# Attention weights turned compact and set on the diagonal by DMA, with the patch products moved

## The chip, the cores and the metric

One core of a Trainium2 chip. Its engines run side by side and wait for each other by semaphores: PE (TensorE, matrix products, results in PSUM), DVE (VectorE), ACT (ScalarE), POOL (GpSimd), and SP (SyncE), whose queue issues most DMA transfers. The metric is the device time of one launch in microseconds (us), the median of several runs.

## What is computed

A vision transformer layer on 64 images: patches are embedded (36 patches and one class token, so 37 tokens of 256), attention with 16 heads of 64, a layer norm, a mixture of 8 experts with two chosen per token plus a shared feed-forward part, and a second layer norm. Cut to what the change touches:

```python
def _L0_attn_ref(x, Wq, Wkv, Wout, b_out, pos_emb):
    B, N, D = x.shape                      # 64, 37, 256
    ...
    sim = jnp.einsum('bid,bjd->bij', q, k) * scale
    sim = sim + _cope(q, sim, pos_emb)
    attn = jax.nn.softmax(sim, axis=-1)    # 37 x 37 for each image and head
    out = jnp.einsum('bij,bjd->bid', attn, v)
    ...
    return out @ Wout + b_out
```

Everything is in float32.

## The kernel before

**Tiling.** Three images make a group `g` of 111 rows (3 x 37); there are 22 groups, the last with one image. Two groups make a pair `p` (0 to 10): groups `2p` (called `a = 0` or `ga`) and `2p + 1` (`a = 1` or `gb`). Pairs 2 to 9 run as a hardware loop or in the same form; pair 0, pair 1 and pair 10 are written apart. After pair 10 come the router and the shared part (PE lines 1060 to 1293), then the experts in tiles of 128 tokens (lines 1360 and 1372), then the second norm and the output.

**One pair on PE**, in the order in which it is written by hand (`pair` in the tensor block): `queries(p)` (line 878), `score(p, 0)` (957), `values(p, 0, ·)` (971), `turn_weights(2p - 1)` (993), `values(p, 1, ·)`, `outputs(2p - 1)` (1006), `score(p, 1)`, `embed(p + 1)` (869, the patch products), `residual(p - 1)` (1015), `keys(p + 1)` (878), `turn_weights(2p)`, `by_tokens(p - 1)` (1031), `outputs(2p)`. Each engine runs its own list in its own order; a semaphore wait stops everything that stands behind it on that engine.

**How the attention weights get to the output product.** `softmax_norm` on DVE (lines 1888 to 1900) sums the exponentials `ex`, takes the reciprocal, multiplies it by `own_f` (one where a row belongs to image `b`, zero elsewhere), and writes `attn[row, head, image, token]`, 111 x 16 x 111, in four parts of four heads: so each head's 111 x 111 block is zero outside the three 37 x 37 diagonal blocks. PE turns each head by a product with the identity (16 of them a group), ACT copies the four banks to `attnT` (line 1476), and PE multiplies the values `v_sb` by `attnT`, one product a head, 111 rows deep.

**Around it.** ACT takes every PSUM result away: `score` (three copies one after another, 1435 to 1439), `values` (1470), `gates` (1455 and 1457, what the next scan on DVE starts from), `outputs` (1491), `keys` (1420), `queries` (1415), `split` (1524), `softmax_exp` (1499). DVE carries `cope`, the position term, in seven parts for each group: a scan (1827) that waits for `gates`, shifted copies by predicate (1844), and arithmetic up to `lg` (1868), from which ACT takes the exponential. `embed(p + 1)` on DVE (1815) stands behind part 7 of `cope(ga)`. DVE's first step for group `ga` is `tables_out` (1912), which waits for `score(p, 0)` on PE. SP issues `save_h` (574), `store_rows` (562), `store_halves` (569), `load_x` (557), `turn_x` (610, a transposing DMA) and `back_h` (582) for each pair; behind the loop it loads the rows for the router (`load_rec`, 641) and the experts' weights (656, 659).

## Time and profile before

| | |
|---|---|
| median of 3 runs | 718.61 us (717.4 to 719.63) |
| the profiled execution's own time | 717.29 us |
| its span, first to last instruction | 715.5 us |
| mean granted PE clock | 0.994 |
| busy: PE, DVE, ACT, POOL | 98%, 73%, 61%, 17% |

Of the span, pairs 0 to 10 take about 477 us, the rest of the router and the shared part runs to 540 us, the experts to 657 us. The profile's views used below are: the timeline (start, length, engine, line, what is written from what, and in square brackets how long the engine sat idle before it and who ended that), the busy time in given stretches (which also gives the granted PE clock, 1.00 being 2.4 GHz and 0.50 being 1.2 GHz), the list of the instructions of one tile, and the DMA view.

### The profile page before, as it was taken

The numbers are of one execution on the slowest core, as the hardware profiler recorded it, in microseconds if no ns is written. First come the engines' busy times: TensorE is split into PE (matmuls) and PEld (weight loads), VectorE is DVE, ScalarE is ACT, GpSimd is POOL, SyncE is SP. The second block draws the span as 40 slices with busy tenths as digits, with TensorE's granted clock in tenths as the row PEclk, the third lists the DMA queues.
The fourth block names the chain that finished last, engine by engine and source line by source line (L and its number), as shares of the span: only waits on it lengthen the run. The fifth ranks groups of instructions, "written<-read, shape, count | busy, mean of one in ns | idle before, by whom it ended". The sixth has DMA issues, their size and how long they took to land. (4 is left out here: it accounts for less than half of the span.)

```text
span 715.5 us, 14500 instructions
## 1 busy us (share of the span) xinstructions
PE 698.0 (98%) x4930; PEld 606.4 (85%) x4931; DVE 524.1 (73%) x1109; ACT 437.4 (61%) x772; POOL 122.0 (17%) x158
## 2 busy tenths in 40 slices
PE   8999999999999999999999999989998999999995
PEld 5897897979889797988979796868887999998884
DVE  3378998989989898989989898986862222332657
ACT  1565777676776867677686747543216777784453
POOL 2000000000000000000000000010024777775130
PEclk9999999999999999999999999989999999999999
DMA  8620040402304040210402003920004655542811
GB/s 272 225 64 0 2 102 26 102 20 43 76 13 102 25 101 25 61 53 13 94 21 64 25 25 115 345 77 25 3 26 97 146 136 132 147 130 57 287 69 54
DMA packets 75659, 60.79 MB, mean 85 GB/s; under 512 B 49386, under 2 KB 66896, under 8 KB 75628
## 3 DMA queue, kind: packets, MB, share of 16 engines
q1 hardware_dynamic: 71056, 50.35, 26.0%
q0 software_dynamic: 4224, 9.71, 5.1%
q8 instruction: 17, 0.28, 0.2%
q10 hardware_dynamic: 348, 0.34, 0.1%
q14 instruction: 14, 0.11, 0.0%
HBM read 35.40 MB, written 15.54 MB: 71 GB/s over the span
## 5 line engine op out<-in xcount | busy, mean ns | idle before, releaser
L1360 PEld LDWEIGHTS ps_S<-attnT,v_sb 128*128 128x128 f32 x704 | 84.8, 192 | 5.8 <-ACT attnT L1691 3.4
L1360 PE MATMUL ps_S<-attnT,v_sb 128*128 128x128 f32 x704 | 85.8, 275 | 2.5 <-ACT attnT L1691 2.5
L1844 DVE COPY_PREDICATED table<-bit,table 111x112 f32<-111x112 int16 (+6 forms) x110 | 75.0, 682 | 11.2
L775 POOL TENSOR_TENSOR rs<-ve,neg_half 111x2 f32<-111x2 f32 x11 | 12.2, 1113 | 402.4 <-DVE ve L1936 402.4
L971 PE MATMUL ps_X<-wkv_sb,hT 128*111 128x512 f32 (+1 forms) x176 | 80.6, 598 | 0.0
L2280 DVE COPY attnT<-ps_S 128x256 f32<-128x256 f32 x44 | 18.7, 424 | 80.9 <-PE ps_S L1372 80.8
L1015 PE MATMUL ps_X<-oT,wout_sb 128*128 128x222 f32 x320 | 62.0, 350 | 0.0
L1015 PEld LDWEIGHTS ps_X<-oT,wout_sb 128*128 128x128 f32 x320 | 60.0, 190 | 0.0
L878 PE MATMUL ps_S<-hT,wq_sb 128*128 128x216 f32 (+1 forms) x320 | 59.2, 342 | 0.0
L971 PEld LDWEIGHTS ps_X<-wkv_sb,hT 128*111 128x111 f32 (+1 forms) x176 | 28.5, 173 | 35.0 <-issue 34.2
L878 PEld LDWEIGHTS ps_S<-hT,wq_sb 128*128 128x128 f32 x320 | 56.1, 189 | 1.3
L794 POOL DMA_INDIRECT attn<-hh_d,ids_x x44 | 45.2, 1026 | 60.6 <-issue 57.0
L1711 ACT COPY v_sb<-gu_sb 128x1024 f32 x44 | 45.7, 1038 | 12.2 <-issue 8.1
L957 PE MATMUL ps_S<-kT,qT 64*111 64x150 f32 (+1 forms) x704 | 50.5, 293 | 0.0
L957 PEld LDWEIGHTS ps_S<-kT,qT 64*111 64x111 f32 (+1 forms) x704 | 45.0, 170 | 5.5 <-issue 2.9
L1900 DVE TENSOR_TENSOR attn<-ex,rdo 111x444 f32<-111x444 f32 x84 | 46.5, 615 | 2.4
L808 POOL DMA_INDIRECT y_d<-attnT,ids_y x44 | 44.7, 1017 | 18.3 <-issue 10.7
L869 PE MATMUL ps_X<-patT,tokT 128*128 128x216 f32 x240 | 47.7, 353 | 0.0
L869 PEld LDWEIGHTS ps_X<-patT,tokT 128*128 128x128 f32 x240 | 44.2, 188 | 1.7 <-issue 1.7
L1372 PE MATMUL ps_S<-down_sb,q 128*128 x176 | 45.2, 380 | 0.3 <-DVE q L2274 0.3
L1691 ACT COPY attnT<-table 128x512 int16<-128x512 int16 x44 | 33.7, 766 | 18.8 <-DMA table<-attn 18.7
L993 PEld LDWEIGHTS ps_S<-ident,attn 111*111 111x111 f32 x336 | 35.7, 177 | 10.1 <-DVE attn L1900 6.3
(319 smaller groups left out, 1391.4 us busy)
## 6 DMA issues: line engine op xcount, KB each, us to landing
down_sb<-in_x_dram SPq DMA_DIRECT2D x10, 648.0 KB
gu_sb<-y_d SPq DMA_DIRECT2D x8, 512.0 KB, 6.5
h_d<-hT SPq DMA_DIRECT2D x11, 222.0 KB, 2.6
kept<-h_d SPq DMA_DIRECT2D x11, 222.0 KB, 2.8
h_d<-h SPq DMA_DIRECT2D x10, 222.0 KB
wkv_sb<-in_L_attn_Wkv_dram SPq DMA_DIRECT2D x2, 1024.0 KB, 12.5
gu_sb<-in_L_ffn_gate_w_dram SPq DMA_DIRECT2D x2, 1024.0 KB, 9.7
gu_sb<-in_L_ffn_up_w_dram SPq DMA_DIRECT2D x2, 1024.0 KB, 11.1
```

The source lines that it names most:

```text
L794: nc.gpsimd.indirect_dma_start(xg[:, b], None, hh_d[:, :], bass.IndirectOffsetOnAxis(ap=ids_x[:, t:t + 1], axis=0), bounds_check=REAL - 1, ...
L808: nc.gpsimd.indirect_dma_start(y_d[:, :], bass.IndirectOffsetOnAxis(ap=ids_y[:, t:t + 1], axis=0), y_sb[:, b], None, bounds_check=TOPK * R ...
L869: mm = nc.tensor.matmul(embedded(p, m), tokT[:, k, m * P:(m + 1) * P], pt[:, k % 2, :, :, k // 2, :], start=(k == 0), stop=(k == KP - 1))
L878: mm = nc.tensor.matmul(bank[:, i * NPAT:i * NPAT + n * (TOK - 1)], w[:, k, c:c + P], hT[:, k, :n, 1:], start=(k == 0), stop=(k == KE - 1))
L957: mm = nc.tensor.matmul(S[lane:lane + r, bank, col:col + KW], qT[part, f, a * ROWS:a * ROWS + r], kT[part, f, a], start=True, stop=True)
L971: mm = nc.tensor.matmul(X[:r, 1 - s], hT[:, k].rearrange("p b t -> p (b t)")[:, a * ROWS:a * ROWS + r], wkv_sb[:, k, INNER + 512 * s:INNER ...
L1015: mm = nc.tensor.matmul(bank[:, m * COLS:m * COLS + w], wout_sb[:, f, m * P:(m + 1) * P], oT[:, f, :w], start=(f == 0), stop=(f == FT - 1))
L1360: mm = nc.tensor.matmul(S[:, i, j * FF + f * P:j * FF + f * P + P], held[:, i, k, j, f * P:f * P + P], xgT[:, i, k], start=(k == 0), stop= ...
L1372: mm = nc.tensor.matmul(E[:, i, :EMB], hid[:, i, k * P:(k + 1) * P], down_sb[:, bass.ds(e, 1), k].rearrange("p o f -> p (o f)"), start=(k ...
L1711: nc.scalar.copy(held[:, i].rearrange("p k j f -> p (k j f)"), gu_sb[:, bass.ds(e, 1)].rearrange("p o k j f -> p (o k j f)")).then_inc(til ...
L1844: A.did(V.copy_predicated(near[:, :, :, 0:SL - d], by_side(bit[:, n], r)[:, :, :, 0:SL - d], near[:, :, :, d:SL]))
L1900: V.tensor_tensor(attn[:r, of], ex[:r, of].unsqueeze(2).to_broadcast(by_head), rdo[:r, of].unsqueeze(3).to_broadcast(by_head), ALU.mult).t ...
```

## The change

**Compact weights.** DVE writes the softmax without zeros: one product `attn[row, head, token]`, 111 x 16 x 37, with each head padded to 40 columns (`own_attn`). `own_f` and its product are gone. PE turns three heads at a time: 120 columns become 120 rows, in 6 products with the identity a group (five of three heads, one of a single head) where there were 16. ACT copies two banks of three products each to `turned_attn` (two copies of 120 x 333 for four of 111 x 444). Nine DMAs on SP (`place_attn`), each of 40 rows and 6 or 5 heads (888 or 740 bytes a row), then set the three images' blocks on the diagonal of `own_T`, which lies in `attnT`, 120 rows deep. POOL zeroes `attnT` once. `outputs` waits for the nine (`placed[a]`). The values (`v_sb`, `hT`, `kept`, `h_d`) get the same padding to 40 tokens an image, 120 rows a group; the last group, with one image, keeps the old form.

**Order.** PE: `embed(p + 1)` now stands ahead of `outputs(2p - 1)`, writing to bank `S[:, 2]`; `turn_weights(2p)` stands behind the first of the four key products; `outputs(2p)` moves into the next pair, ahead of the fourth query product; for group 0 it stands behind `patches(2)`, for group 20 behind three products of the shared part. ACT: `weights(2p - 1)` ahead of `gates(p, 0)`; `softmax_exp(2p)` ahead of `gates(p, 1)`; `distance(2p)` and `halves_of_x` earlier; the two halves of `turned_patches` among the query copies of the next pair. DVE: `embed(p + 1)` behind part 4 of `cope(ga)` instead of part 7. SP: the nine transfers of each group, and behind the loop the experts' weights after them.

On ACT, in the loop, between the copies of the scores and the gates. `v_sb` is a copy of value products, `th` and `gate` are the gates. Before:

```order
L1439 COPY simS<-ps_S 37x666
L1470 COPY v_sb<-ps_X 111x512
L1455 ACTIVATE th<-simS 111x592
L1457 ACTIVATE gate<-th 111x16x37
L1470 COPY v_sb<-ps_X 111x512
```

and after:

```order
L1487 COPY simS<-ps_S 37x666
L1518 COPY v_sb<-ps_X 120x512
L1523 ISA
L1524 COPY attn<-ps_S 120x3x111
L1523 REGISTER_ALU
L1524 COPY attn<-ps_S 120x3x111
L1503 ACTIVATE th<-simS 111x592
L1505 ACTIVATE gate<-th 111x16x37
L1518 COPY v_sb<-ps_X 120x512
```

Two copies of turned weights, with their waits for PE, now stand between the scores and the gates.

On PE, in the loop, from the turned weights of `gb` to the second score. Before:

```order
L993 MATMUL ps_S<-ident,attn 111x111 x4
L967 REGISTER_ALU
L971 MATMUL ps_X<-wkv_sb,hT 111x512 x4
L1006 MATMUL ps_S<-attnT,v_sb 64x111 x16
L957 MATMUL ps_S<-kT,qT 111x150 x6
```

and after:

```order
L1036 MATMUL ps_S<-ident,attn 120x111 x5
L1036 MATMUL ps_S<-ident,attn 40x111
L1009 REGISTER_ALU
L1014 MATMUL ps_X<-wkv_sb,hT 120x512 x4
L907 ISA
L911 MATMUL ps_S<-patT,tokT 128x216 x12
L1053 MATMUL ps_S<-attnT,v_sb 64x111 x16
L999 MATMUL ps_S<-kT,qT 111x150 x6
```

The patch products (`patT,tokT`) now lie between the value products and the output products.

On SP, in the loop, from the load of the next patches (`load_x`) to the end of the loop's body. Before:

```order
L555 REGISTER_ALU
L557 ISA
L557 DMA down_sb<-in_x_dram 108x1536
L608 ISA
L610 DMA_TRANSPOSE gu_sb<-down_sb 128x24x112
L579 ISA
L582 DMA kept<-h_d 128x444
```

and after:

```order
L645 DMA_TRANSPOSE gu_sb<-down_sb 128x24x112
L631 REGISTER_ALU
L632 ISA
L637 DMA attnT<-attn 40x222 x3
L637 DMA attnT<-attn 40x185 x6
L599 ISA
L602 DMA kept<-h_d 128x480
```

The nine transfers of a group stand ahead of `back_h`, behind a wait for ACT's copies.

The diff, cut to its core:

```diff
+            def place_attn(p, a):
+                g = p * 2 + a
+                if first(g):
+                    sp.wait_ge(attnT_zeroed, 1)
+                else:
+                    sp.wait_ge(o_done, g * 2)
+                sp.wait_ge(at_sb, g * 4 + 4)
+                apart(sp)
+                for j in range(TPG):
+                    n, at = in_block[j], from_slot[j]
+                    for b in range(TPG):
+                        sp.dma_start(own_T[PAD * b:PAD * b + PAD, b, at:at + n], turned_attn[PAD * j:PAD * j + PAD, b, :n]
+                                     ).then_inc(placed[a], 16)
...
             with sp.Fori(2, G2 - 4) as p:
                 save_h(p)
                 store_rows(p - 2)
+                place_attn(p - 1, 1)
                 store_halves(p - 2)
                 load_x(p + 3, XR)
                 turn_x(p + 2)
+                place_attn(p, 0)
                 back_h(p)
...
             for c in range(4, FULL):
                 load_rec(c)
+            place_attn(G2 - 2, 1)
             store_halves(G2 - 3)
+            back_h(G2 - 1)
+            place_attn(G2 - 1, 0)
+            store_rows(G2 - 2)
+            load_rec(FULL)
...
             def queries(p, ahead):
...
+                    if s == 3 and not next_first(p):
+                        outputs(p * 2 - 2, 0)
...
             def keys(p):
...
+                    if s == 1 and not next_first(p):
+                        turn_weights(p * 2 - 2, True)
...
             def turn_weights(g, ahead):
...
-                for j, s in enumerate(IN_TURN):
-                    pe.wait_ge(attn_ready, g * 4 + j + 1)
-                    for i in range(4):
-                        mm = nc.tensor.transpose(S[:r, s, i * r:i * r + r], attn[:r, 4 * s + i], ident[:r, :r])
-                    mm.then_inc(at_done, 1)
+                pe.wait_ge(attn_ready, g * 4 + 4)
+                for n in range(BLOCKS):
+                    heads_in = attn_flat[:r, heads_of(n)]
+                    mm = nc.tensor.transpose(S[:heads_in.shape[1], n // 3, n % 3 * r:n % 3 * r + r], heads_in, ident[:r, :r])
+                    if n % 3 == 2:
+                        mm.then_inc(at_done, 2)
...
             def outputs(g, a):
                 r = rows_of(g)
+                if r == ROWS:
+                    pe.wait_ge(placed[a], (g - a) * (8 * PLACES) + 16 * PLACES)
...
             def first_pair():
...
-                pe.wait_ge(q_sb, 4 + 2)
+                pe.wait_ge(q_sb, 4 + 3)
                 turn_weights(0, True)
+                values(1, 0, 0)
                 pe.wait_ge(q_sb, 4 + 4)
-                outputs(0, 0)
+                pe.wait_ge(at_sb, 4)
                 patches(2)
...
             def pair(p, ahead):
                 if next_first(p):
-                    values(p, 0, 0)
+                    outputs(0, 0)
...
                 values(p, 1, 1)
-                if not ahead:
+                if ahead:
+                    embed(p + 1)
+                else:
                     pe.wait_ge(h1t_sb, 1)
                 outputs(p * 2 - 1, 1)
                 score(p, 1)
...
-                outputs(p * 2, 0)
-                if not ahead:
                     pe.wait_ge(at_sb, 4 * (G - 1))
                     for j in range(2):
                         shared_part(0, 0, j)
+                    shared_part(0, 1, 0)
+                    outputs(p * 2, 0)
...
             def weights(g):
-                for j, s in enumerate(IN_TURN):
-                    act.wait_ge(at_done, g * 4 + j + 1)
-                    nc.scalar.copy(attnT[:ROWS, 4 * s:4 * s + 4, :ROWS],
...
+                for j in range(2):
+                    act.wait_ge(at_done, g * 4 + 2 * j + 2)
+                    nc.scalar.copy(turned_attn[:TPG * PAD, :, 3 * j:3 * j + 3],
...
             def packed_norm(g):
...
-                dve.wait_ge(at_done, g * 4)
+                dve.wait_ge(placed[0], 16 * PLACES * G2)
...
             def softmax_norm(g):
...
-                N.did(V.tensor_tensor(rdo[:r], rden[:r].unsqueeze(2).to_broadcast([r, HEADS, TPG]),
-                                      own_f[:r].unsqueeze(1).to_broadcast([r, HEADS, TPG]), ALU.mult))
...
-                for s in IN_TURN:
-                    of = slice(4 * s, 4 * s + 4)
-                    V.tensor_tensor(attn[:r, of], ex[:r, of].unsqueeze(2).to_broadcast(by_head),
...
+                V.tensor_tensor(own_attn[:r, :, :TOK], ex[:r], rden[:r].unsqueeze(2).to_broadcast([r, HEADS, TOK]), ALU.mult
+                                ).then_inc(attn_ready, 4)
...
-                    if ahead and part == 7:
+                    if ahead and part == (7 if first(p) else 4):
                         embed(p + 1)
```

## Rows read from the trace of the kernel before

**Rows 1.** The page, busy time, share and count of each engine.

```profile
PE 698.0 (98%) x4930; PEld 606.4 (85%) x4931; DVE 524.1 (73%) x1109; ACT 437.4 (61%) x772; POOL 122.0 (17%) x158
```

**Rows 2.** Timeline of PE, pairs 2 and 5: start, length, line, count, idle before.

```profile
101.67 6.12 PE L878 MATMUL ps_S<-hT,wq_sb 128*128 128x216 f32 x32
...
225.48 6.12 PE L878 MATMUL ps_S<-hT,wq_sb 128*128 128x216 f32 x32
231.53 2.30 PE L957 MATMUL ps_S<-kT,qT 64*111 64x150 f32 x32
...
237.40 1.81 PE L993 MATMUL ps_S<-ident,attn 111*111 111x111 f32 x16
239.04 3.60 PE L971 MATMUL ps_X<-wkv_sb,hT 128*111 128x512 f32 x8
```

**Rows 3.** Timeline of DVE over one pair.

```profile
211.40 0.77 DVE L1868 TENSOR_TENSOR lg<-nb,mx 111x592 f32<-111x592 f32 x1
212.10 1.02 DVE L1815 TENSOR_TENSOR hT<-ps_X,posb 128x216 f32<-128x216 f32 x2
213.01 0.77 DVE L1888 TENSOR_REDUCE den<-ex 111x16 f32<-111x592 f32 x1
...
214.44 2.21 DVE L1900 TENSOR_TENSOR attn<-ex,rdo 111x444 f32<-111x444 f32 x4
216.57 0.80 DVE L1922 SCALAR_TENSOR_TENSOR resT<-ps_X,posT,kept 128x222 f32<-128x222 f32 x2
...
233.87 0.89 DVE L1912 COPY table<-ps_S 111x702 f32<-111x702 f32 x1 [0.31 <-PE ps_S L957]
...
239.02 1.46 DVE L1827 TENSOR_TENSOR_SCAN u<-scan_keep,gate 111x624 f32<-111x624 f32 x1 [0.71 <-ACT gate L1457]
```

**Rows 4.** Timeline of ACT, from the gates to the weights' copies.

```profile
237.56 0.70 ACT L1455 ACTIVATE th<-simS 111x592 f32<-111x592 f32 x1
...
240.40 1.82 ACT L1476 COPY attnT<-ps_S 111x444 f32<-111x444 f32 x4
```

**Rows 5.** Timeline of PE and of DVE around the start of pair 1.

```profile
60.22 1.72 PE L993 MATMUL ps_S<-ident,attn 111*111 111x111 f32 x16
...
63.63 1.33 PE L859 MATMUL ps_S<-ident,down_sb 108*128 108x108 f32 x12
...
68.96 0.89 DVE L1912 COPY table<-ps_S 111x702 f32<-111x702 f32 x1
```

**Rows 6.** Timeline of SP's queue, PE and DVE in pair 10.

```profile
440.94 3.55 SPq L641 DMA_DIRECT2D wq_sb<-h_d  x3
...
447.91 1.70 PE L1006 MATMUL ps_S<-attnT,v_sb 111*64 111x111 f32 x30
...
459.17 0.80 DVE L1922 SCALAR_TENSOR_TENSOR resT<-ps_X,posT,kept 128x222 f32<-128x222 f32 x2
...
468.24 0.38 PE L1073 MATMUL ps_S<-tokT,rw_sb 128*8 128x256 f32 x1
...
472.53 1.13 PE L1091 MATMUL ps_S<-tokT,sgu_sb 128*128 128x256 f32 x4
...
476.31 0.89 PE L986 MATMUL ps_S<-ident,attn 101*37 101x101 f32 x8 [2.65 <-DVE attn L1882]
```

**Rows 7.** Stretches: length, busy (count) of PE, PEld, DVE, ACT, POOL, clock, DMA.

```profile
477.00:480.00 3.00, 3.00 (x39) 2.41 (x36) 2.10 (x8) 1.29 (x4) 0.96 (x1) 0.63 0.16 59
...
484.00:486.00 2.00, 2.00 (x15) 2.00 (x14) 0.00 (x0) 0.00 (x0) 0.00 (x0) 0.84 0.16 56
...
535.00:540.00 5.00, 3.21 (x15) 1.61 (x13) 1.11 (x3) 1.48 (x2) 1.61 (x2) 1.00 0.88 151
```

**Rows 8.** Tile views of `hh_d` and `h_d`; DMA view of 199 to 205 us.

```profile
L569 SPq DMA_DIRECT2D hh_d<-halves_b x10: 245/246/347, 116.9 to 481.5; - x10
...
DMA to landing us min/median/max: 2.0/2.8/9.3
...
DMA packets 228, 0.23 MB, mean 38 GB/s; under 512 B 6, under 2 KB 228, under 8 KB 228
```

More of the change, by code:

```diff
@@ L146, in vit_tower @@
         rden = sb("rden", [P, HEADS])
-        rdo = sb("rdo", [P, HEADS, TPG])
         attnT = sb("attnT", [P, HEADS, ROWS])
+        attn_flat = attn[:].rearrange("p h b j -> p (h b j)")
+        own_attn = attn_flat[:, :HEADS * PAD].rearrange("p (h j) -> p h j", h=HEADS)
+        BLOCKS = -(-HEADS // TPG)
+        in_block = [len(range(j, HEADS, TPG)) for j in range(TPG)]
+        from_slot = [sum(in_block[:j]) for j in range(TPG)]
+        turned_attn = (attn_flat[:, HEADS * PAD:HEADS * PAD + BLOCKS * TPG * TOK]
+                       .rearrange("p (b n q) -> p b n q", b=TPG, n=BLOCKS))
+        own_T = attnT[:].rearrange("p h r -> p (h r)").rearrange("p (b h q) -> p b h q", b=TPG, h=HEADS)
         oT = sb("oT", [P, FT, COLS])
@@ L330, in vit_tower @@
         o_done = sem("o_done")
+        attnT_zeroed = sem("attnT_zeroed")
+        placed = [sem(f"placed_{a}") for a in range(2)]
         ot_sb = sem("ot_sb")
@@ L781, in _ @@
             regroup(1)
+            nc.gpsimd.memset(attnT[:], 0.0).then_inc(attnT_zeroed, 1)
+            pool.wait_ge(attnT_zeroed, 1)
             pool.wait_ge(xt_done, 9)
@@ L789, in _ @@
             pool.wait_ge(at_done, 4 * G)
+            pool.wait_ge(placed[0], 16 * PLACES * G2)
             nc.gpsimd.memset(xg_flat, 0.0).then_inc(xg_zeroed, 1)
@@ L1171, in pair @@
                 score(p, 1)
-                if ahead:
-                    pe.wait_ge(v_ready, p * 4 + 4)
-                    embed(p + 1)
                 pe.wait_ge(v_ready, p * 4 + 3)
@@ L1190, in pair @@
                         turn(c)
-                turn_weights(p * 2, True)
+                if not ahead:
+                    turn_weights(p * 2, True)
                 if ahead:
@@ L1588, in pair @@
                         queries(p, s)
-                if not next_first(p):
-                    for s in range(2, 4):
-                        queries(p, s)
+                        if not last(p):
+                            turned_patches(p + 1, s)
+                    queries(p, 2)
+                    outputs(p * 2 - 2, 0)
+                    queries(p, 3)
                 if ahead:
@@ L1597, in pair @@
                     softmax_exp(p * 2 - 1)
+                else:
+                    weights(p * 2 - 1)
                 gates(p, 0)
@@ L1601, in pair @@
                     split(p - 2)
-                weights(p * 2 - 1)
-                if not ahead:
+                if ahead:
+                    distance(p * 2)
+                    if ahead2:
+                        halves_of_x(p + 2)
+                else:
+                    weights(p * 2 - 1)
                     turn(0)
@@ L1607, in pair @@
                     values(p, 1, s)
-                distance(p * 2)
+                if not ahead:
+                    distance(p * 2)
                 score(p, 1)
                 tables_out(p, 1)
+                if ahead:
+                    softmax_exp(p * 2)
                 gates(p, 1)
-                if not ahead:
+                if ahead:
+                    keys(p + 1, 0)
+                    weights(p * 2)
+                    for s in range(1, 4):
+                        keys(p + 1, s)
+                    distance(p * 2 + 1)
+                else:
                     for c in range(1, 3):
                         turn(c)
-                softmax_exp(p * 2)
-                if ahead2:
-                    halves_of_x(p + 2)
-                if ahead:
-                    for s in range(4):
-                        keys(p + 1, s)
-                else:
+                    softmax_exp(p * 2)
                     for c in range(3, FULL):
                         turn(c)
-                weights(p * 2)
-                distance(p * 2 + 1)
-                outputs(p * 2, 0)
-                if ahead2:
-                    turned_patches(p + 2)
+                    weights(p * 2)
+                    distance(p * 2 + 1)
+                    outputs(p * 2, 0)
             act.dma_start(pe_nat[:TOK, :], pos_embed[0]).then_inc(w_small, 16)
```

132 lines of the change are left out of this document (66 added, 66 removed).

## The prediction, made before the kernel ran

> **What bounds the kernel now.** First the page's shares: PE is busy 98% of the span, DVE 73% [rows 1]. That looks as if every matrix product removed came off the time. The timeline by pairs says more. A pair takes (225.48 - 101.67)/3 = 41.27 us on PE [rows 2]. In the same pair DVE waits only twice: 0.31 us for PE's score, at its copy of the table, and 0.71 us for ACT's gate, at its scan [rows 3]. So DVE's own chain is about 41.27 - 0.38 = 40.9 us long (the table's wait with some overlap taken off; the other one comes back below). PE is the bound by half a microsecond, and whatever it gives up beyond that turns into waiting for DVE. The profiled execution took 717.29 us, 1.8 more than its span and 1.3 less than the median; the sum is made on it and the 1.3 added at the end. A measurement of this kernel can tell about 0.3%, 2.15 us, from no change.
>
> **PE's savings.** The 16 products of a turn take 237.40 to 239.04, 1.64 us, 0.1025 each [rows 2]. Six remain of them, so a pair loses 20 x 0.1025 = 2.05 us of PE. Padding to 120 rows adds no column that a product moves, so it costs PE nothing. PE's need falls to 39.2 us a pair, and about 40.0 with two waits that come with the new order: about 0.6 for the second value product, whose bank ACT now empties behind the gates, and 0.2 for a key product, whose copy stands behind the turned weights on ACT.
>
> **DVE's chain, step by step, a pair.**
> - Norm: one product without zeros takes the place of the four of 444 columns and of `rdo`. Before, from `den` at 213.01 to `resT` at 216.57, 3.56 us [rows 3]. The new product has 592 elements a row, as `den` has, so 0.77 us like it; with `den` and the reciprocal 1.79. That is -1.77 for `ga`. For `gb` it is nothing: that norm stands ahead of the scan, which waits for the gate, and the wait only grows, to some 3.3 us.
> - The gates come later: ACT now copies the turned weights of `gb` first, two copies of 120 x 333 for which the four of 444, 1.82 us together [rows 4], bound one at 0.35 to 0.46. The first copy can begin some 0.5 us behind the start of the turn (three products and the semaphore), so `th` starts about 1.3 behind it, at 238.4 instead of 237.56 [rows 4]: +0.84. What ACT queues behind this wait are both gates and the second value copy, and who waits is DVE's scan.
> - `embed(p + 1)` covered the wait for the exponential: it ran from 212.10 between `lg` (end 212.17) and `den` at 213.01 [rows 3]. At part 4 it costs its own time and the gap of 0.84 behind `lg` stays: about +0.87.
> - The wait for the score at the table, with its overlap, is gone: -0.38.
> Sum -0.44, so 40.83 us a pair, DVE the bound, PE ahead by 0.7 to 0.8. I take -0.40 a pair for nine pairs, **-3.6 us**, a few hundredths of waiting being likely to stay.
>
> **The nine transfers.** The nearest rows: a store of 111 rows occupies SP's queue 0.25 to 0.35 us, and a transfer lands 2.0 us after issue at least, 2.8 in the median, 9.3 at most [rows 8]. So from ACT's last copy to `placed` it is 0.2 + 8 x 0.33 + 2.3 = **5.1 us**. The low end, with issues of 0.25, is 4.3. For the high end I let the packets be the limit: in the stretch with both `hh_d` stores, 228 packets took about 4.1 us, 55 a microsecond [rows 8]; 360 packets then take 6.5 us, and with the landing 8.8. I take 5.1, since the rows of issue are nearest to what is done here. The rate of 228 packets may be one of few engines, as the DMA share of 0.16 beside other transfers hints [rows 7]. The Trainium skill, "DMA: Bandwidth & Descriptors", section "Why a DMA increments its semaphore by 16 and not by 1", says that the number of engines is the largest up to 16 that divides the row count: 3 for 111 rows, 8 for 40. By that rule the 360 packets would take an estimated 2.4 us, hidden behind the issue, and the sum would stay with 5.1; no row here shows a 40-row transfer.
>
> **Where it is hidden.** In the loop 3.6 us of value products [rows 2] and 4.6 of patch products stand between the turn of `gb` and its outputs, against about 1.5 + 5.1 needed; for `ga`, three key and three query products, 9 us. On SP `back_h` and the next store stand behind the nine, with the transposing transfer ahead of them; that needs the halves of x, which ACT now makes before the outputs. Nothing there comes last.
>
> **Where it is exposed: three places.**
> - *Group 0.* The turn starts at 60.22 [rows 5], is done at 60.84, copied at 61.6, placed at 66.7. PE has values (1.8) and patches (1.2, [rows 5]) and is through at 63.8: 2.9 us idle. Outputs 1.7 and score 2.3 follow, and DVE's table of pair 1 comes at 70.7 instead of 68.96 [rows 5]: **+1.75**. DVE enters pair 10 at +1.75 - 3.6 = -1.85.
> - *Group 19.* SP becomes free at 440.94 + 3.55 - 1.85 = 442.6 [rows 6], the copies are there by 442.4, so placed at 447.8: outputs as before at 447.91 [rows 6], PE idle about 4 us. The 1.85 is used up here for the residual; `resT` comes 0.4 earlier only.
> - *Group 20.* `resT` at 458.8 instead of 459.17 [rows 6], 0.8 for it and 1.79 for the norm: attention ready at 461.4, turned at 462.3, copied at 463.1, placed at 468.3. PE is through with what stands ahead at 466.05: 2.2 us idle. Outputs to 470.0, their copies 0.75, then the products that ran from 468.24 to 472.53 before [rows 6], 4.3 us: the last group's turn comes at 475.1. Before, it came at 476.31, behind 2.65 us of idling for DVE [rows 6]. So **-1.2**, and from there PE's chain is dense to the experts: the end moves one for one. The second place and the third make the first forget much; all three together, a microsecond of latency is worth up to 3 us of time.
>
> **PE's clock.** After the 2.65 us of idling the granted clock was 0.63 in 477 to 480 and 0.84 in 484 to 486, in between at the 1.2 GHz level; that cost about 3.1 us. An idle stretch of 1.8 us in 535 to 540 left it at 1.00 [rows 7]. So idle stretches near 2 us are safe here, near 2.7 not always. The new ones: 2.9 us (chance 0.55 of a fall), 4 us (0.85), 2.2 us (0.3); and the old one is gone or shorter (0.6). Likeliest: both longer stalls bring a fall, the old fall goes: +2.3 + 2.8 - 3.1 = **+2.0**.
>
> **The small edits** are nothing: the weights' loads of the experts begin at 474 instead of 445 and are needed at 534 or later; POOL, which zeroes `attnT`, is idle at 17% [rows 1]; two more small memsets on DVE at the start, +0.1 at most. If the loads' cover were gone, the experts would wait their landing, up to 9.3 us [rows 8].
>
> **Sum.** -1.2 + 2.0 = +0.8: the profiled execution at 718.1, the median at **719.4**; with L from 4.6 to 5.6 and the clock's falls one more or less 716.5 to 722.
>
> **Rivals.**
> - *The clock holds at the new stalls*, and falls nowhere: -1.2 - 3.1 = -4.3, 714.3. For it: most short idle stretches leave it at 1.00. Against it: 4 us is longer than any in the pairs. With a latency at its low end, 1 us better still. Chance 0.26.
> - *The nine transfers are slow* (the other side). Place: the three above, and with it the outputs of `gb` in the loop. Price: 3 us a microsecond; at 7 us it is +6, at 8.8, beyond the loop's cover of 8.15 + 0.6 - 1.5 = 7.2, some +11: 725 to 731. It decides from about 6 us. For it: landings of up to 9.3. Chance 0.17.
> - *ACT's order costs more than 0.84* a pair: the weights' copies wait for the turn, which waits for the norm of `gb` and for the value products; half a microsecond more a pair is +4.5, 724. Chance 0.08.
> - *PE is the bound after all*, DVE's 40.9 holding slack that the rows don't show, and the products removed count in full: 10 pairs x 2.05 less, +2 to +4 at the stalls: about 702. Against it: the two waits of DVE, 0.31 and 0.71. Chance 0.07.
> The forecast itself has 0.42.
>
> **How the numbers follow.** The range must leave out no more than 0.2: it reaches from below the clock rival with a shorter latency, 712.0, to 727.5, a latency of 7.5 us; outside are the PE case and the slow end of the transfers, and a share of the tails. Faster than 716.45: 0.24 of the clock rival, 0.07, 0.02 of the forecast: 0.33. Slower than 720.75: 0.17, 0.08 and 0.12 of the forecast: 0.37. The rest, 0.30, is no difference to be told.
>
> **What would show it.** A pair of 40.8 us with DVE waiting about 3.3 for the gate and 0.8 for the exponential, and PE waiting about 0.6 for a bank of values. PE idle for 2.9, 4 and 2.2 us ahead of outputs near 64, 444 and 466. Nine issues of 0.33 and a landing of 2.3 behind the last. A granted clock of 0.5 near 67 and 449, none near 477. It would be wrong if a pair took 41.3 or 39.5, if the placements took over 6 us, or if the clock's falls were elsewhere.

## The result, and the profile after

The changed kernel takes 741.6 us in the median of 4 runs (741.1 to 744.6), the kernel before 718.0 beside it: a ratio of 1.034, 95% interval 1.030 to 1.037. It is 3.4% slower, where 719.4 and a range of 712 to 727.5 had been forecast. The profiled execution has a span of 740.1 us, 24.6 more than before, and the profile's page says that it is not work: PE, DVE and ACT are all busy for less time than in [rows 1], POOL for 0.8 us more.

```profile
PE 690.8 (93%) x4720; PEld 590.9 (80%) x4721; DVE 489.3 (66%) x1027; ACT 418.5 (57%) x730; POOL 122.8 (17%) x156
```

So the time is idling. The timeline of PE (start, length, engine, line, what from what, and in brackets the idle time ahead and who ended it) has four long stretches of it that the kernel before did not have:

```profile
70.49 3.23 PE L1053 MATMUL ps_S<-attnT,v_sb 120*64 120x111 f32 x32 [6.10 <-DMA attnT<-attn]
...
461.39 3.23 PE L1053 MATMUL ps_S<-attnT,v_sb 120*64 120x111 f32 x32 [5.69 <-DMA attnT<-attn]
...
487.64 3.00 PE L1053 MATMUL ps_S<-attnT,v_sb 120*64 120x111 f32 x32 [5.13 <-DMA attnT<-attn]
...
497.76 0.89 PE L1029 MATMUL ps_S<-ident,attn 101*37 101x101 f32 x8 [0.43 <-DVE attn L1939]
...
522.23 0.38 PE L1129 MATMUL ps_S<-ident,qT 8*128 8x8 f32 x2 [4.02 <-ACT qT L1558]
522.97 6.62 PE L1341 MATMUL ps_S<-sdown_sb,v_sb 128*128 128x256 f32 x16
```

Before, the last of these lines was

```profile
500.35 3.72 PE L1293 MATMUL ps_S<-sdown_sb,v_sb 128*128 128x256 f32 x16
```

The first three are the three places of the prediction, with 6.1, 5.7 and 5.1 us of idling instead of 2.9, 4 and 2.2. The fourth is not in it at all. And behind each the products are slow: 32 output products take 3.23, 3.23 and 3.00 us where they take 1.74 elsewhere, and the 16 of line 1341 take 6.62, for 3.72 before. The turn of the last group, ahead of which the kernel before idled 2.65 us and lost its clock ([rows 6], [rows 7]), now waits 0.43 us and runs at full speed. In 70 to 75 us the granted clock is at its 1.2 GHz level, 0.51 in the seventh column:

```profile
70.00:75.00 5.00, 4.51 (x44) 4.24 (x46) 0.00 (x0) 1.66 (x3) 0.00 (x0) 0.51 0.00 1
```

Why the placements are late stands in SP's queue, here for the second group of a pair:

```profile
246.87 6.88 SPq L637 DMA_DIRECT2D attnT<-attn  x9
254.03 0.28 SPq L589 DMA_DIRECT2D hh_d<-pe_full  x1
254.58 0.25 SPq L589 DMA_DIRECT2D hh_d<-halves_b  x1
```

Nine issues take 6.88 us, 0.76 each with the gap; the stores behind them take 0.28 and 0.25, as in [rows 8]. The tile's list gives the issue as 706 ns, at least and in the median, over all 189: each costs that much, and not one now and then.

```profile
L637 SPq DMA_DIRECT2D attnT<-attn x189: 706/706/884, 62.3 to 485.7; - x189
...
DMA to landing us min/median/max: 2.1/2.5/2.7
```

The landing is what was forecast (2.3), the issue is not. From the end of ACT's last copy to the output products it is 8.2 us instead of 5.1: 0.1 to the first issue, 8 x 0.76 to the ninth, 2.1 for its landing. For group 0 ACT's two copies end at 62.21 and the outputs begin at 70.49, 8.28 later; for groups 19 and 20 it is 8.22 and 8.11. (The expectations of the experiments take 8.8, which counts nine issue times where eight lie between the first and the last.)

```profile
61.43 0.78 ACT L1524 COPY attn<-ps_S 120x333 f32<-120x333 f32 x2
...
246.00 0.78 ACT L1524 COPY attn<-ps_S 120x333 f32<-120x333 f32 x2 [0.33 <-PE ps_S L1036]
```

In the loop the same latency is just hidden: from 246.78, the end of the copies, to 255.03, where PE is through with the value and patch products and begins the outputs, is 8.25 us.

```profile
255.03 1.74 PE L1053 MATMUL ps_S<-attnT,v_sb 120*64 120x111 f32 x32
```

In the loop the copy of DVE's table is at 241.89 and, a pair later, at 283.18: 41.29 us, to compare with 41.27 in [rows 2]. The 2.05 us that PE saves a pair are there in the rows and not in the time:

```profile
245.41 0.78 PE L1036 MATMUL ps_S<-ident,attn 111*120 111x111 f32 x6
...
248.62 1.98 PE L1014 MATMUL ps_X<-wkv_sb,hT 128*120 128x512 f32 x4 [0.70 <-ACT v_sb L1518]
...
272.82 4.73 PE L920 MATMUL ps_S<-hT,wq_sb 128*128 128x216 f32 x24 [0.62 <-ACT kT L1468]
```

and on DVE:

```profile
248.13 1.46 DVE L1884 TENSOR_TENSOR_SCAN u<-scan_keep,gate 111x624 f32<-111x624 f32 x1 [3.42 <-ACT gate L1505]
...
264.11 0.77 DVE L1945 TENSOR_REDUCE den<-ex 111x16 f32<-111x592 f32 x1 [0.76 <-ACT ex L1547]
264.91 0.25 DVE L1947 RECIPROCAL rden<-den 111x16 f32<-111x16 f32 x1
265.36 0.78 DVE L1951 TENSOR_TENSOR attn<-ex,rden 111x592 f32<-111x592 f32 x1 [0.20 <-DVE rden L1947]
```

The waits for the gate (3.3 forecast) and for the exponential (0.8) are where they were expected.

Where the 24.6 us arise, by the same step in both traces. The forecast's column has falls of the clock only in its last row.

| step | before | after | later by | forecast |
|---|---|---|---|---|
| DVE's table of pair 1 | 68.96 | 76.59 | 7.6 | 1.75 |
| DVE's table of pair 10 | 440.55 | 448.70 | 8.15 | -1.85 |
| outputs of group 19 | 447.91 | 461.39 | 13.5 | -0.1 |
| turn of the last group | 476.31 | 497.76 | 21.45 | -1.2 |
| router's turned sums, line 1129 | 499.89 | 522.23 | 22.3 | |
| shared products behind them | 503.91 | 529.43 | 25.5 | |
| end of the span | 715.5 | 740.1 | 24.6 | 0.8 |

From the last turn to the router's sums only 0.85 us are added, though PE idles 4.02 us there: the fall of the clock that the kernel before had at this turn is gone.

### The profile page after: what moved, and what is told of

It is laid out like the page before. It is cut to its first block, busy times and chain, and to the rows that moved or that the text cites. A ratio compares the mean times of both kernels' runs of the same rounds, so it can differ in the third digit from the quotient of the medians.

```text
span 740.1 us, 14154 instructions
## 1 busy us (share of the span) xinstructions
PE 690.8 (93%) x4720; PEld 590.9 (80%) x4721; DVE 489.3 (66%) x1027; ACT 418.5 (57%) x730; POOL 122.8 (17%) x156
## 4 chain that ended last, share of the span: by engine, by line
PE 79%; SPq 7%; DMA 5%; ACT 5%; issue 3%; DVE 1%; ACTq 0%; DVEq 0%; POOLq 0%
PE ps_S L920 13%; PE ps_S L1408 10%; PE ps_X L1062 8%; PE ps_X L1014 7%; PE ps_S L999 7%; PE ps_S L1138 6%; PE ps_S L1420 5%; PE ps_S L1053 5%; PE ps_S L911 5%; SPq L637 4%; PE ps_S L1341 4%; PE ps_X L920 2%; PE ps_S L929 2%; PE ps_S L1036 1%; SPq L706 1%
## 5 line engine op out<-in xcount | busy, mean ns | idle before, releaser
L1014 PE MATMUL ps_X<-wkv_sb,hT 128*120 128x512 f32 (+1 forms) x176 | 83.1, 604 | 6.3 <-ACT v_sb L1518 6.3
L920 PE MATMUL ps_S<-hT,wq_sb 128*128 128x216 f32 (+1 forms) x320 | 62.5, 347 | 5.2 <-ACT kT L1468 5.2
L1014 PEld LDWEIGHTS ps_X<-wkv_sb,hT 128*120 128x120 f32 (+1 forms) x176 | 28.9, 179 | 43.5 <-issue 28.9
L1053 PE MATMUL ps_S<-attnT,v_sb 120*64 120x111 f32 (+1 forms) x704 | 41.9, 276 | 17.4 <-DMA attnT<-attn 17.4
L1053 PEld LDWEIGHTS ps_S<-attnT,v_sb 120*64 120x64 f32 (+1 forms) x704 | 37.0, 147 | 24.2 <-DMA attnT<-attn 15.1
L999 PE MATMUL ps_S<-kT,qT 64*111 64x150 f32 (+1 forms) x704 | 52.5, 301 | 0.0
L1884 DVE TENSOR_TENSOR_SCAN u<-scan_keep,gate 111x624 f32<-111x624 f32 (+1 forms) x22 | 31.3, 1422 | 30.8 <-ACT gate L1505 30.8
L1539 ACT COPY oT<-ps_S 128x444 f32<-128x444 f32 (+1 forms) x44 | 22.3, 531 | 42.8 <-PE ps_S L1053 42.8
L920 PE MATMUL ps_S<-hT,wkv_sb 128*128 128x216 f32 x232 | 44.9, 348 | 0.0
```

The source lines that it names most:

```text
L920: mm = nc.tensor.matmul(bank[:, i * NPAT:i * NPAT + n * (TOK - 1)], w[:, k, c:c + P], hT[:, k, :n, 1:TOK], start=(k == 0), stop=(k == KE - 1))
L999: mm = nc.tensor.matmul(S[lane:lane + r, bank, col:col + KW], qT[part, f, a * ROWS:a * ROWS + r], kT[part, f, a], start=True, stop=True)
L1014: mm = nc.tensor.matmul(X[:keyed, 1 - s], hT[:, k].rearrange("p b t -> p (b t)")[:, at:at + keyed], wkv_sb[:, k, INNER + 512 * s:INNER + 5 ...
L1053: mm = nc.tensor.matmul(S[odd * DH:odd * DH + DH, 4 + half, f % 4 * ROWS:f % 4 * ROWS + r], v_sb[:keys_of(r), a, h * DH:h * DH + DH], weights,
```

## Experiments

The kernel before ran again beside each set of experiments, with medians from 716.9 to 718.4 us; the ratios are to those.

**What an issue costs.** In `place_attn` the nine transfers became nine of different forms:

```diff
-                for j in range(TPG):
...
+                sp.dma_start(own_T[:40, 0, a0:a0 + 6], turned_attn[:40, 0, :6]).then_inc(placed[a], 16)
+                sp.dma_start(own_T[40:80, 1, a0:a0 + 1], turned_attn[:40, 1, :1]).then_inc(placed[a], 16)
+                sp.dma_start(own_T[80:112, 2, a0:a0 + 6], turned_attn[:32, 2, :6]).then_inc(placed[a], 16)
+                sp.dma_start(own_T[:16, 0, a1:a1 + 5], turned_attn[40:56, 0, :5]).then_inc(placed[a], 16)
...
```

> The nine transfers of each group are replaced by nine of different forms, each once: 40 rows of 888 bytes as in the change, 40 rows of 148 bytes, 32, 16 and 8 rows, 40 rows to DRAM, 40 rows from DRAM, 120 rows, 37 rows. The attention weights are therefore not the right ones; the output is not the reference's. In the changed kernel each of the 189 issues occupies SP's queue for at least 0.706 us, where a store of 111 rows to DRAM takes 0.25. Theory A (both ends in SBUF make the issue slow): the issues to and from DRAM take 0.25 to 0.4, all others about 0.7 whatever their rows and bytes. Theory B (the number of rows decides, by how it splits over DMA engines): 32 and 16 rows take 0.25 to 0.4, and 40 rows 0.7 also to and from DRAM. Theory C (packets under 1 KB, or their number): 8 rows are cheaper than 40, and 120 rows dearest.

The list of each line's instructions (least, median and most ns of 21): 40 rows of 888 bytes, 40 rows of 148 bytes, 32 rows, 16 rows, 8 rows, 40 rows to DRAM, 120 rows, 40 rows from DRAM, 37 rows.

```profile
L637 SPq DMA_DIRECT2D attnT<-attn x21: 765/796/909, 62.1 to 486.1; - x21
L638 SPq DMA_DIRECT2D attnT<-attn x21: 720/732/767, 63.0 to 486.9; - x21
L639 SPq DMA_DIRECT2D attnT<-attn x21: 555/559/584, 63.8 to 487.7; - x21
L640 SPq DMA_DIRECT2D attnT<-attn x21: 578/590/594, 64.5 to 488.3; - x21
L641 SPq DMA_DIRECT2D attnT<-attn x21: 665/665/666, 65.1 to 489.0; - x21
L642 SPq DMA_DIRECT2D scrap_d<-attn x21: 453/460/461, 65.8 to 489.7; - x21
L643 SPq DMA_DIRECT2D attnT<-attn x21: 860/887/900, 66.3 to 490.2; - x21
L644 SPq DMA_DIRECT2D attnT<-in_L_attn_Wq_dram x21: 497/504/505, 67.2 to 491.1; - x21
L645 SPq DMA_DIRECT2D attnT<-attn x21: 646/651/657, 67.8 to 491.7; - x21
```

No theory holds alone. The bytes of a row don't matter (796 and 732, the first of a row of issues being dearer). Both ends in SBUF cost 0.2 to 0.3 over one end in DRAM with the same 40 rows, as A said, but one end in DRAM is still 0.46 to 0.50, not 0.25. Rows count a little, and not steadily: 32 and 16 rows 0.56 to 0.59, 37 rows 0.65, 8 rows 0.67, 120 rows 0.89, only 0.09 to 0.18 more than 40. What decides is the number of transfers: three of 120 rows would be issued in an estimated 2.7 us (3 x 0.89), nine of 40 take 6.9. What makes the difference between 0.25 for a store of 111 rows and 0.46 for one of 40 stays open.

**Latency.** Three of the nine transfers only:

```diff
-        PLACES = TPG * TPG
+        PLACES = TPG
...
-                for j in range(TPG):
+                for j in range(1):
```

> Of the nine transfers of a group only three are made (the first three heads' block for each image); the rest of the attention weights stays zero or old, so the output is not the reference's. Theory (nine issues of 0.75 in a row make the latency of 8.8 us, which is exposed ahead of the outputs of groups 0, 19 and 20): the latency becomes 4.5, each stall shrinks by 4.3 to about 1.8, 1.4 and 0.8 us, no fall of the clock follows (2.1 + 2.9 + 3.4 us), and a pair in the loop keeps its 41.3 us. The time falls from 741.6 by 13 + 8 = 21, to about 721. Rival (the stalls are made up elsewhere, since DVE is the bound): under 8 us are gained, over 733.

Measured: 725.0 us, 1.013 of the kernel before (1.008 to 1.017), 16.6 less than the changed kernel. The idle time ahead of the three outputs is 1.64, 2.04 and 0.67 us:

```profile
65.46 1.74 PE L1053 MATMUL ps_S<-attnT,v_sb 120*64 120x111 f32 x32 [1.64 <-DMA attnT<-attn]
...
450.35 1.74 PE L1053 MATMUL ps_S<-attnT,v_sb 120*64 120x111 f32 x32 [2.04 <-DMA attnT<-attn]
...
469.26 1.74 PE L1053 MATMUL ps_S<-attnT,v_sb 120*64 120x111 f32 x32 [0.67 <-DMA attnT<-attn]
...
476.94 1.47 PE L1029 MATMUL ps_S<-ident,attn 101*37 101x101 f32 x8 [0.94 <-DVE attn L1939]
...
504.98 0.38 PE L1129 MATMUL ps_S<-ident,qT 8*128 8x8 f32 x2 [5.98 <-ACT qT L1558]
```

The outputs run at 1.74 again, and the turn of the last group is at 476.94, 20.8 ahead of the changed kernel: the theory's 21. Then 4.2 are given back: the clock falls at this turn (8 products 1.47 us, 0.89 at the full level), and the fourth stretch of idling grows from 4.02 to 5.98. Six issues less, 4.6 us, are worth 20.8 us at the end of the attention part, so a microsecond of latency is worth 4.6 us and not the 3 of the prediction: 12.6 of the 20.8 are the three stalls, shorter by 4.46, 3.65 and 4.46, and most of the rest is the clock, as the extra products below show.

**The fourth stall.** The experts' weights behind the last stores on SP (the loads of `gu_sb` and `down_sb`, moved as they stand):

```diff
             load_rec(FULL + 1)
-            sp.wait_ge(xt_sb, 3 * G2)
...
             store_halves(G2 - 2)
...
                 sp.dma_start(hh_d[row:row + r, :], h1_halves[a][:r]).then_inc(hh_stored[a], 16)
+            sp.wait_ge(xt_sb, 3 * G2)
...
```

> The loads of the experts' weights stand behind all stores on SP instead of ahead of the last ones; nothing else changes. In the changed kernel ACT waited 3.66 us for the store of the halves, which was issued at 509 behind the loads, PE then idled 4.02 us and its clock fell for 3 us of work. Theory (the order of the loads on SP is the cause): that stall and the fall go, the loads still land ahead of the experts: 741.6 - 6 = 735 to 736. Rival (something else is late next, as the chain of the last group, or the weights then land too late): no gain, or slower.

Measured: 733.0 us, 1.021 (1.019 to 1.023), 8.6 less than the changed kernel, more than the 6 expected. The prediction had called the move free, because the weights are not needed before 534. It had not asked what stands behind them. In the changed kernel's queue the stores of the halves (line 589) follow the experts' loads, and take ten and seven times as long to issue as in the loop:

```profile
502.42 6.63 SPq L709 DMA_DIRECT2D down_sb<-in_L_ffn_down_w_dram  x2
509.09 2.91 SPq L589 DMA_DIRECT2D hh_d<-pe_full  x1
512.04 1.83 SPq L589 DMA_DIRECT2D hh_d<-halves_b  x1
```

ACT waits for the first of them to reuse its buffer, and with its next copy holds up the router's turned sums on PE:

```profile
519.05 0.62 ACT L1572 COPY pe_full<-h 111x512 int16<-111x512 int16 x1 [3.66 <-DMA hh_d<-pe_full]
```

The kernel before shows the same, at another place: there the load of `kept` came behind these loads, and took 3.31 us to issue, where the median of the eleven is 0.39.

```profile
460.69 3.31 SPq L582 DMA_DIRECT2D kept<-h_d  x1
```

So a row of the kernel before gave the price of standing behind the weights. With the stores first, the timeline of PE has neither the stall nor the slow products behind it:

```profile
517.13 0.28 PE L1130 MATMUL ps_S<-ident,qT 8*128 8x8 f32 x2
...
517.59 3.72 PE L1342 MATMUL ps_S<-sdown_sb,v_sb 128*128 128x256 f32 x16
```

**The clock.** Products whose results nobody reads, ahead of the three late outputs:

```diff
+            def keep_busy(n):
+                for _ in range(n):
+                    nc.tensor.matmul(S[:, 4], ident[:, :], wout_sb[:, 0:2, :].rearrange("p f e -> p (f e)"),
+                                     start=True, stop=True)
...
                 if next_first(p):
+                    keep_busy(12)
                     outputs(0, 0)
```

> 12, 11 and 10 products of 512 columns whose results nobody reads are added on PE ahead of the outputs of groups 0, 19 and 20, in the idle stretches of 6.1, 5.7 and 5.1 us. Theory (the granted clock falls after these idle stretches, and the fall costs 2.1, 2.9 and 3.4 us): the clock stays at 1.00 there, the waits themselves stay, and the time falls by 6 to 8 us to 734 to 736. Rival (the clock is not what made the products behind them slow, or DVE absorbs it): within 1 us of 741.6.

Measured: 749.3 us, 7.7 more than the changed kernel. This one was mis-sized: a product of 512 columns takes 0.87 us (two instructions of 0.44), so 12 of them filled 10.5 us where 6.1 were idle, and put the outputs off themselves. The granted clock was 1.00 in all three places all the same. With half as many:

```diff
-                    keep_busy(12)
+                    keep_busy(6)
```

> The extra products of e4, half as many: 6, 5 and 5 calls of 512 columns, since one took 0.87 us and not 0.45. They end ahead of the placements, so that they add nothing to the chain. Theory (the clock's falls after the three long stalls cost 2.1, 2.9 and 3.4 us): the outputs of groups 0, 19 and 20 take 1.74 us instead of 3.2, the granted clock is 1.00 behind them, and the time falls from 741.6 to 733 to 736, less what the later stall for the stores gives back. Rival (the clock costs nothing that the later waits don't take up): 740 to 742.

Measured: 736.7 us, 1.029 (1.026 to 1.032), 4.9 less than the changed kernel.

```profile
64.33 5.33 PE L1160 MATMUL ps_S<-wout_sb,ident 128*128 128x512 f32 x12
70.59 1.74 PE L1053 MATMUL ps_S<-attnT,v_sb 120*64 120x111 f32 x32 [0.93 <-DMA attnT<-attn]
...
517.23 0.38 PE L1129 MATMUL ps_S<-ident,qT 8*128 8x8 f32 x2 [6.81 <-ACT qT L1567]
```

The outputs of group 0 begin when they did (70.59 and 70.49), but run at full clock. At the turn of the last group it is 7.8 us ahead of the changed kernel (489.97 against 497.76): that is the price of the clock's falls at the three stalls, expected as 8.4. 2.8 of it is lost again at the fourth stall, which is 6.81 us now: whatever is gained ahead of a queue that is late anyway, waits there.

**Was DVE the bound of the kernel before?** Its own form, with 6 of the 16 turning products:

```diff
                     pe.wait_ge(attn_ready, g * 4 + j + 1)
-                    for i in range(4):
+                    for i in ((0, 1), (0,))[j // 2]:
```

> The kernel before, with 6 of the 16 products that turn a group's attention weights and the 10 others left out (their heads get old bank contents, so the output is not the reference's); nothing else changes. It measures what 2.05 us less of PE a pair is worth while DVE does all it did. If PE alone is the bound: 41.27 - 2.05 = 39.2 us a pair and 717.5 - 20 = 697. If DVE's chain is 40.9 us, as the prediction had it: a pair of 40.9 with PE waiting for DVE, and 713 to 715.

Measured: 713.5 us, 0.995 (0.994 to 0.997), and DVE's tables of two pairs at

```profile
193.41 0.88 DVE L1912 COPY table<-ps_S 111x702 f32<-111x702 f32 x1
234.31 0.88 DVE L1912 COPY table<-ps_S 111x702 f32<-111x702 f32 x1
```

40.90 us apart, with PE waiting 0.38 and 0.18 for `attn` and 0.54 for `attnT`. This part of the prediction stands: taking 20 us of products off an engine that is busy 98% of the span brings 3.4.

**Who bounds the loop of the changed kernel?** A wait on PE moved to where it is needed:

```diff
                     if s == 3 and not next_first(p):
+                        pe.wait_ge(k_sb, p * 4 + 4)
                         outputs(p * 2 - 2, 0)
...
-                if ahead:
-                    pe.wait_ge(k_sb, p * 4 + 8)
-                else:
+                if not ahead:
                     pe.wait_ge(h1t_sb, FULL)
```

> One wait on PE is moved in the changed kernel: for the copy of the last key bank, from ahead of the first query product to ahead of the outputs behind the third, which are the first to write that bank. In the changed kernel PE idles there 0.62 us a pair. Theory A (the loop of 41.29 us is PE's own ring: 39.9 us of products, 0.6 more than planned since interrupted series cost time, and 1.33 us of waits for ACT's copies): a pair takes 40.7 and the time falls by 5 to 6, to 736. Theory B (DVE is the bound, the step of the prediction was only sized wrong by 0.45): a pair stays at 41.2 to 41.3, the time within 1 us of 741.6.

Measured: 740.1 us (1.032, interval 1.030 to 1.035), which the intervals do not tell from the changed kernel, but a pair of (282.78 - 241.69) = 41.09. The 0.62 us of idling is gone from its place and 0.58 stand at the next one, ahead of the turn:

```profile
245.22 0.78 PE L1037 MATMUL ps_S<-ident,attn 111*120 111x111 f32 x6 [0.58 <-ACT simS L1486]
```

That turn waits for ACT's copies of the scores, which follow DVE's table. So neither theory as it was put. Call a ring the chain of steps and waits that comes back to its start a pair later: the two rings are 0.2 us apart, PE's at 41.29 and DVE's at 41.09. The same 0.2 us stand ahead of DVE's table: it begins 0.93 us behind the start of the step before it in the changed kernel (240.96 and 241.89), and 0.69 behind it here.

**ACT's order.** The gates ahead of the turned weights, in `pair` on ACT:

```diff
-                else:
-                    weights(p * 2 - 1)
                 gates(p, 0)
+                if ahead:
+                    weights(p * 2 - 1)
                 values(p, 0, 1)
```

> On ACT the gates stand ahead of the copies of the turned weights again, as in the kernel before; the rest is the changed kernel. DVE's scan gets its gate 0.9 us earlier, the weights land 1 us later. Theory A (PE's ring is the bound, and nine issues of 0.75 leave the placements of the second group only some 1 us of cover): PE waits 0.5 to 2 us a pair for the placements, a pair of 41.8 to 43, the time 746 to 757. Theory B (DVE is the bound): a pair of 40.4 to 40.8, the time 733 to 737.

Measured: 748.9 us, 1.044 (1.042 to 1.047), a pair of 42.17. DVE's wait for the gate is 2.32 instead of 3.42, and PE now waits in each pair for what landed in time before:

```profile
259.40 1.74 PE L1053 MATMUL ps_S<-attnT,v_sb 120*64 120x111 f32 x32 [1.23 <-DMA attnT<-attn]
```

A microsecond of DVE's ring can't be had while the nine transfers are issued by one queue. That is theory A's mechanism in its range, though not because PE alone bounds the loop.

**Two queues.** Four of the nine transfers on POOL:

```diff
+        BY_POOL = [(1, 2), (2, 0), (2, 1), (2, 2)]
+        PLACES = TPG * TPG - len(BY_POOL)
...
+                for j, b in BY_POOL:
+                    n, at = in_block[j], from_slot[j]
+                    nc.gpsimd.dma_start(own_T[PAD * b:PAD * b + PAD, b, at:at + n], turned_attn[PAD * j:PAD * j + PAD, b, :n]
+                                        ).then_inc(placed_too[a], 16)
```

> Four of the nine transfers of every group are issued by POOL's queue, five by SP's; the work is the same. Theory (the latency of 8.8 us is nine issues of 0.75 in a row on one queue): with 5 on SP it is 5 x 0.75 + 2.1 + 0.2 = 6.0 us, if POOL needs no more than 1 us for each of its four; the three stalls of 6.1, 5.7 and 5.1 us shrink by 2.8 each, and with fewer falls of the clock the time is 741.6 - 8 to -16: 726 to 733. Rival (what lasts is the transfer itself, or POOL's issues are dearer than SP's): over 737.

Measured: 735.6 us, 1.025 (1.022 to 1.028). POOL issues one in 0.512 us, SP's five take 3.8. The stalls are 5.17, 3.50 and 2.10 us instead of 6.10, 5.69 and 5.13. The first is the odd one: POOL was at a memset until 65.6 there, so its four came late. And the fourth stall took its share again, 7.51 us.

**All of it together.** The changed kernel with five transfers on POOL's queue and four on SP's, the first group's ahead of that memset, the stores ahead of the experts' weights, the moved wait, and on ACT the gates and the second value copy ahead of the turned weights. Beside the edits of e3, e6 and e8:

```diff
-                else:
-                    weights(p * 2 - 1)
                 gates(p, 0)
                 values(p, 0, 1)
+                if ahead:
+                    weights(p * 2 - 1)
...
+        BY_POOL = [(1, 1), (1, 2), (2, 0), (2, 1), (2, 2)]
...
+            place_share(0, 0)
             pool.wait_ge(xt_done, 9)
```

> The changed kernel with all causes that the runs named taken away: five of the nine transfers on POOL's queue, four on SP's; the experts' weights behind the last stores; the wait for the last key bank moved to the outputs; on ACT the gates and the second value copy ahead of the turned weights. Theory: a pair of 40.3 to 40.6 us (DVE's ring is 0.95 shorter by the earlier gates and 0.2 by the moved wait), so 6 to 9 us over nine pairs; 8.6 us by the order of the stores; latency 5.5 us instead of 8.8, three stalls shorter by 3.3. In all 741.6 - 8.6 - 10 - 7 = about 715 to 718, no slower than the kernel before. Rival (the placements of the second group, 2 us later by ACT's order, are not hidden): a pair of 41 or more, over 722.

Measured: 713.8 us in 5 runs, 0.995 of the kernel before (0.993 to 0.997), 27.8 less than the changed kernel.

```profile
67.04 1.74 PE L1080 MATMUL ps_S<-attnT,v_sb 120*64 120x111 f32 x32 [2.68 <-DMA attnT<-attn]
...
191.45 0.88 DVE L1987 COPY table<-ps_S 111x702 f32<-111x702 f32 x1
231.53 0.88 DVE L1987 COPY table<-ps_S 111x702 f32<-111x702 f32 x1
...
235.05 0.78 PE L1062 MATMUL ps_S<-ident,attn 111*120 111x111 f32 x6 [0.59 <-ACT simS L1512]
...
236.67 1.46 DVE L1909 TENSOR_TENSOR_SCAN u<-scan_keep,gate 111x624 f32<-111x624 f32 x1 [2.26 <-ACT gate L1530]
```

A pair takes 40.08 us, 1.2 less than in either kernel: from table to scan DVE needs 5.14 where it needed 6.24. The loop gives 11 us, more than expected, the stalls are 2.68, 1.94 and 1.62 us, and no output product right behind them is slow. So the change can be made a gain of 4.6 us, 0.6%. It is not more for two reasons. In the loop PE now waits 0.59 us a pair for what follows DVE's table. And DVE's table of pair 10 comes 8.8 us ahead of the kernel before (431.79 against 440.55), but the outputs of group 19 only 4.9 ahead (442.98 against 447.91):

```profile
436.98 0.66 PE L1134 MATMUL ps_S<-ident,wkv_sb 128*128 128x128 f32 x4 [1.52 <-DMA wkv_sb<-h_d]
437.56 3.48 PE L1040 MATMUL ps_X<-wkv_sb,hT 128*37 128x512 f32 x4
...
442.98 1.74 PE L1080 MATMUL ps_S<-attnT,v_sb 120*64 120x111 f32 x32 [1.94 <-DMA attnT<-attn]
```

PE waits there for the router's rows and then for the placements, whose issues on SP begin at 436.76, behind the loads of those rows. From SP's first issue to the outputs it is 6.2 us there, and 4.8 and 4.5 at groups 0 and 20. Between the two waits the clock fell (0.50 in 439 to 441), so four value products took 3.48 us for 1.91 in the changed kernel. Whether another place for those loads would give the 3.8 us back was not tried, and neither was what the new order on ACT and PE would bring without compact weights.

And with the extra products of e9 in it, 3, 3 and 2 of them:

```diff
                 if next_first(p):
+                    keep_busy(3)
                     outputs(0, 0)
```

> The kernel of e10 with 3, 3 and 2 of the extra products of e9 ahead of the three outputs, to hold the clock over stalls of 2 to 3.5 us. Theory: 2 to 5 us faster than e10, 711 to 715, faster than the kernel before by up to 0.7%. Rival: the stalls of e10 are too short for the clock to fall, and the two are equal.

Measured: 713.8 us in 11 runs (710.6 to 716.6), 0.994 (0.992 to 0.996): the rival. Behind these three stalls of 2.7 us and less there was no fall left to prevent; the one at the turn of the last group, which the kernel before has too ([rows 7]), is in both traces.

## Why the prediction was wrong, point by point

- **The bound of the kernel before** (DVE's chain of 40.9 us behind a PE at 98%): right, e5 measured 40.90. That the products removed are not worth 20 us was right with it.
- **The nine transfers**: the step that failed. The term 8 x 0.33 took the issue of a store of 111 rows to DRAM as the nearest row. Measured are 8 x 0.76, so the latency was 8.2 and not 5.1; the landing (2.3 forecast, 2.1 to 2.7) was right. The upper end of 8.8 came near by accident: it was a rate of packets, and e1 shows that packets are not it. The estimate by the rule of the Trainium skill ("DMA: Bandwidth & Descriptors", section "Why a DMA increments its semaphore by 16 and not by 1") took 8 engines for 40 rows; the largest divisor of 40 up to 16 is 10, which makes it an estimated 2.0 us instead of 2.4. No run shows the number of engines, and the difference changes nothing, since the issue was the limit. Why this form costs 0.71 and a store of 111 rows 0.25 stays open. The rival that the transfers are slow, with 0.17, is what happened. Its price of 725 to 731 was too low, as 3 us a microsecond was.
- **Where it is hidden**: right, with nothing to spare. The loop's cover was put at 7.2 us and is 8.25, against a latency of 8.2; e7 takes a microsecond of it away and PE waits 1.23.
- **The price of latency**: the three places were the right three. With 3.1 us more each, the prediction's own way of counting gives 9.3. By the turn of the last group the difference to its column is 21.45 + 1.2 = 22.65 us: 5.85 at group 0, 4.15 in the loop (a later point), 3.6 at group 19, 9.05 at group 20. e9 puts 7.8 of them down to the clock at the three stalls, and 9.3 + 4.15 + 7.8 = 21.25. Most of the other 1.4 is that the placements began 0.6 us later than forecast at group 0, whose turn started at 60.82 and not at 60.22, and 0.6 at group 19, where SP and ACT's copies were free later.
- **The loop**: 41.29 a pair, forecast 40.83. Both rings were short by little things. On DVE the gates cost +1.09 instead of +0.84: 1.3 us behind the start of the turn, which [rows 2] has at 237.40, is 238.7 and not the 238.4 of the prediction (measured: 1.25 behind it). And the norm took 1.95 us instead of 1.79, since its last product waits 0.20 for the reciprocal just ahead of it (before, `rdo` stood between). On PE the waits were 1.33 instead of 0.8, and the products, added up from start to start, 39.9 us instead of 39.2: the series that are now cut in two (queries by outputs, keys by the turn) take 0.1 to 0.3 longer each. So 3.6 us for nine pairs became nothing.
- **The clock**: right that idle stretches longer than the 2.65 us of [rows 6] bring a fall, and that the fall at the last turn goes; too cheap, since there were three and a fourth, not two.
- **The small edits**: wrong. The loads moved on SP were costed by when their data are needed, and not by the stores queued behind them. e3 gives 8.6 us for that one change of order. The working looked at what stands behind the nine transfers in the loop, and not at what stands behind the loads here.
- **The range**: it ended at a latency of 7.5 us and left the slow end of the transfers out. The rival for that end came to 731 and no more, since it had no fourth stall and took the 3 us a microsecond of the middle case, without more falls of the clock.

## What to carry to other kernels

Count DMA issues as instructions of their own queue, each at the price of its own kind; a row of another kind is not near enough to take its value. A handful of transfers in a row on one queue is a latency of that many issues, and the next two questions are what else could issue them and what stands behind them. A transfer that is moved on a queue has two prices: when its own data are due, and when those of everything behind it are. Where two engines' rings are within half a microsecond of each other, work taken off one is worth only that half; ask for the other ring's shortest cut first, which here was the order on ACT.

## What the runs showed of the hardware that was not expected

- An issue on SP's queue is not one price: 0.25 to 0.29 us for stores of 111 rows to DRAM, 0.46 for 40 rows to DRAM, 0.50 for 40 rows from DRAM, 0.71 to 0.80 for 40 rows from SBUF to SBUF, 0.56 to 0.59 for 32 or 16 rows, 0.65 for 37, 0.67 for 8, 0.89 for 120. The same transfer on POOL's queue is 0.51. The Trainium skill, "DMA: Bandwidth & Descriptors", section "Anatomy of one DMA — SWDGE (gpsimd) path", gives, for transfers issued by POOL, the sequencer's dispatch as some 50 ns and the making of descriptors as small and variable, and puts most of the fixed 2 us into the receipt. The landings here, 1.7 us at least and 1.8 in the median over both queues in e8, 2.1 to 2.7 on SP's in the changed kernel, are of that size; the 0.51 of an issue on POOL is not.
- A small store behind large loads on the same queue took 2.91 and 1.83 us to issue, for 0.28 and 0.25 in the loop, and held the engine that waited for its buffer for 3.66 us.
- Ahead of the outputs of groups 0, 19 and 20, idle stretches of 0.7 to 2.7 us left the products behind them at full speed (e2, e8, e10), and 3.5 to 6.1 us were each followed by products at the 1.2 GHz level, which cost 2 to 3 us each time (the changed kernel, e8). The length of one idle stretch isn't all: at the turn of the last group the clock fell after 0.94 us (e2), and at the value products of the last pair after 1.52 us (e10), where 1.54 us at the same place left it at 1.00 (e11).
